# Gate logarithms summed by one fp16 product, rewritten instruction orders, and a setup whose ternary comparisons run on GpSimd

## The reference

```python
xn = layernorm(x)
Q, K, V = heads(xn @ Wq.T), heads(xn @ Wk.T), heads(xn @ Wv.T)
g = clip(sigmoid(heads(xn) @ gw.T), 1e-6)               # one gate per token and head
log_c = clip(cumsum(log(g), axis=tokens), -30, 30)       # the gate logarithms
Gc = exp(log_c) + 1e-6
R = silu(K @ sw.T)
S = cumsum(outer(K, V) * R / Gc, axis=tokens) * Gc
attn = (Q @ S) @ Wo.T
w = clip(round(w_latent / scale), -1, 1) * scale          # ternary, scale = mean |row|
h = xn @ w_fc.T + gate * (xn @ v.T @ fast_b.T @ u.T)
ffn = (relu(h) ** 2) @ w_proj.T
out = x + attn + ffn
```

## Time and profile before

| | |
|---|---|
| median of 3 runs | 655.05 us (652.91 to 655.27) |
| the profiled execution, its own time | 652.83 us |
| its span, first to last instruction | 651.0 us |
| mean granted TensorE clock | 0.998 of full |
| PE busy | 629.2 us, 97% |
| PEld (weight loads, beside PE) | 546.5 us, 84% |
| DVE busy | 507.5 us, 78% |
| ACT busy | 435.3 us, 67% |
| POOL busy | 357.1 us, 55% |
| PE's share of the chain that ended last | 92% |

### The profile page before, as it was taken

The page is one execution under the profiler, slowest core; times in us unless marked ns, Lnnn a source line. Parts: engine busy times, 40 slices in busy tenths (PEclk is TensorE's granted clock), DMA queues, the critical chain, the costliest instruction groups (busy, mean ns, idle before and its releaser), DMA issues.

```text
span 651.0 us, 21292 instructions
## 1 busy us (share of the span) xinstructions
PE 629.2 (97%) x7734; PEld 546.5 (84%) x7734; DVE 507.5 (78%) x1245; ACT 435.3 (67%) x999; POOL 357.1 (55%) x434
## 2 busy tenths in 40 slices
PE   3889999999999999999999999999999999999997
PEld 3668888888888888888888888888888888888886
DVE  5998888878787777877778877877787777878673
ACT  2688666767666776766677676667676666767662
POOL 4766465554555555456455555645555554655355
PEclk9999999999999999999999999999999999999999
DMA  9347755666746765554567856667656465677421
GB/s 309 94 124 121 111 140 135 148 142 131 111 117 129 138 132 139 135 119 112 130 139 136 143 130 97 132 136 129 143 130 135 106 125 128 141 128 127 100 45 34
DMA packets 186793, 83.05 MB, mean 128 GB/s; under 512 B 118320, under 2 KB 186160, under 8 KB 186688
## 3 DMA queue, kind: packets, MB, share of 16 engines
q1 hardware_dynamic: 184448, 79.05, 58.3%
q10 hardware_dynamic: 2240, 2.62, 1.2%
HBM read 12.43 MB, written 8.39 MB: 32 GB/s over the span
## 4 chain that ended last, share of the span: by engine, by line
PE 92%; DMA 3%; SPq 2%; DVE 1%; issue 1%; POOL 0%; POOLq 0%; DVEq 0%
PE y_bank L2251 17%; PE attn_bank L2195 9%; PE hid_b L2230 9%; PE hid_a L2230 9%; PE front_b L2132 7%; PE y_bank L2265 7%; PE front_a L2113 6%; PE front_b L2094 6%; PE score_a L2161 5%; PE attn_bank L2209 5%; PE score_b L2161 4%; PE attn_bank L2180 3%; PE hid_a L2232 2%; PE hid_b L2232 2%; DMA x_sb<-in_x 2%
## 5 line engine op out<-in xcount | busy, mean ns | idle before, releaser
L2251 PE MATMUL y_bank<-wproj_t,sq_h 128*128 128x256 f16 x512 | 118.5, 273 | 0.0
L2251 PE MATMUL y_bank<-wproj_t,sq_l 128*128 128x256 f16 x512 | 118.5, 273 | 0.0
L1727 DVE TENSOR_TENSOR sq_l<-relu_sq,sq_h 128x512 f16<-128x512 f32 x128 | 105.3, 824 | 1.0 <-ACT relu_sq L1032 0.9
L1680 DVE TENSOR_TENSOR masked<-score_a,shapes_sb 128x512 f32<-128x512 f32 x128 | 87.0, 680 | 16.0 <-PE score_a L2161 15.9
L1680 DVE TENSOR_TENSOR masked<-score_b,shapes_sb 128x512 f32<-128x512 f32 x128 | 87.2, 681 | 11.8 <-PE score_b L2161 11.7
L666 POOL TENSOR_TENSOR state_diag<-state,state_mask 128x256 f32<-128x256 f32 x56 | 53.4, 954 | 63.6 <-DVE state L1699 63.1
L1032 ACT ACTIVATE relu_sq<-relu_sq 128x512 f32<-128x512 f32 x128 | 79.6, 623 | 9.8 <-DVE sq_l L1727 9.7
L653 POOL COPY decay_halves<-decay 128x1024 uint16<-128x1024 uint16 x32 | 33.2, 1038 | 87.3 <-ACT decay L983 87.3
L697 POOL TENSOR_TENSOR y_both<-y_both,x_sb 128x512 f32<-128x512 f32 x32 | 41.2, 1287 | 70.0 <-DVE y_both L1739 70.0
L1023 ACT ACTIVATE sq_h<-relu_sq 128x512 f16<-128x512 f32 x128 | 79.2, 620 | 0.1
L933 ACT ACTIVATE vg<-front_b 128x304 f32<-128x304 f32 x64 | 27.2, 425 | 71.9 <-PE front_b L2132 71.8
(11 more groups left out here) (189 smaller groups left out, 1662.2 us busy)
## 6 DMA issues: line engine op xcount, KB each, us to landing
q_diag<-q SPq DMA_DIRECT2D x256, 64.0 KB, 2.7
k_stack<-k SPq DMA_DIRECT2D x128, 128.0 KB, 3.8
x_sb<-in_x SPq DMA_DIRECT2D x32, 256.0 KB, 3.3
out_y<-y_both SPq DMA_DIRECT2D x32, 256.0 KB, 3.4
relu_sq<-in_w_fc ACTq DMA_DIRECT2D x1, 1024.0 KB, 11.1
pj_nat<-in_w_proj ACTq DMA_DIRECT2D x1, 1024.0 KB, 13.8
y_both<-in_w_qk ACTq DMA_DIRECT2D x1, 512.0 KB, 4.6
w_stage<-in_w_qkvz_t SPq DMA_DIRECT2D x1, 512.0 KB, 6.3
```

Source lines behind the costliest of these rows:

```text
L1680: nc.vector.tensor_tensor(masked[:, c, g].rearrange("p (h n) -> p h n", h=4), score_bank[g % 2][:].rearrange("p (h n) -> p h n", h=4), cau ...
L1727: nc.vector.tensor_tensor(sq_l[:, q], sq[:, n], sq_h[:, q], ALU.subtract).then_inc(sq_l_done, 1)
L2251: last = mm(y_bank[:, c * D:(c + 1) * D], part[:, q, at:at + P], wproj_t[:, 2 * q + i], start=(q == i == c == n == 0), stop=False, skip_gr ...
```

## The change

- **Logarithms.** `log_high` (ScalarE) and `log_low` (VectorE) split the logarithms, times 1024, into two fp16 halves in one tile. `cumulate` becomes one fp16 product of the triangular matrix against both halves, 64 columns, without the sums before. `sums_taken` (VectorE, a reduction) adds the two halves from PSUM. A DMA on SP's queue (`spread_totals`) spreads the last row of the result, the chunk totals, over all partitions. `sums_before` moves to GpSimd and adds the totals up. `clip_log` becomes two VectorE instructions: add the sums before, then clip.
- **Forms on VectorE.** The two `dens` and the clip go from `tensor_scalar` to `scalar_tensor_tensor` with a second input from SBUF.
- **Ternary setup.** VectorE's `fc_ternary` and `proj_ternary` are gone. GpSimd makes both comparisons (`fc_highs`: 8 more instructions of 256 columns, `proj_highs`: 2 more of 1024). TensorE transposes and subtracts in one go: for each of the 32 blocks one fp16 product with the identity and one with its negative, into the same place.
- **Other setup.** The first unit is transposed by TensorE in place of a DMA (`first_turned`, `first_high`, `first_low`). `columns_low` goes from VectorE to GpSimd. Three of the six big memsets go from GpSimd to VectorE. The values' weights are scaled while they are split.
- **Orders.** The lists of all five engines are new. In the repeated slot the front part works one unit further ahead (`load` 6 ahead, `turn_tokens` 5, `queries_t`, `keys`, `values_gates` 4); the prologue is longer and the epilogue shorter by as much.

```diff
 def cumulate(b, u):
-    pe.wait_ge(before_step, upto(b, u, 2, 0))
-    cum = front_a[:, 0:CH * H]
-    mm(cum, causal_sb, log_den[:].rearrange("p c h -> p (c h)"), start=True, stop=False)
-    mm(cum, ones[:], before[:, u % 2].rearrange("p c h -> p (c h)"), start=False,
+    pe.wait_ge(log_l_done, upto(b, u, 1, 0))
+    mm(front_a[:, 0:2 * CH * H], causal16[:], log16[:].rearrange("p s c h -> p (s c h)"), start=True,
        stop=True).then_inc(cum_full, 1)
...
+def spread_totals(b, u):          # SP
+    sp.wait_ge(sums_taken_done, upto(b, u, 1, 0))
+    last = chunk_sums[P - 1:P, par].rearrange("p c h -> p (c h)")
+    sp.dma_start(totals[:, par].rearrange("p c h -> p (c h)"),
+                 last.unsqueeze(1).to_broadcast([1, P, CH * H])).then_inc(totals_spread[par], 16)
...
+def sums_before(b, u):            # GpSimd
+    pool.wait_ge(totals_spread[par], turned_upto(b, u))
+    nc.gpsimd.tensor_tensor(before[:, par, 1], before[:, par, 0], totals[:, par, 0],
+                            ALU.add).then_inc(before_step, 1)
...
+    nc.gpsimd.tensor_tensor(before[:, 1 - par, 0], before[:, par, 1], totals[:, par, 1],
+                            ALU.add).then_inc(before_step, 1)
...
+def fc_highs(half):               # GpSimd
+    for t in range(HT // 2 * half, HT // 2 * half + HT // 2):
+        last = nc.gpsimd.tensor_scalar(fc_above[:, t], fc_nat[:, t], fc_scale[:, 1, t:t + 1], None,
+                                       ALU.is_gt)
...
 def fc_weights(i):
-    pe.wait_ge(fc_ternary_done, half + 1)
+    pe.wait_ge(fc_below_done, half + 1)
+    pe.wait_ge(fc_above_done, half + 1)
     for j in range(4):
-        last = nc.tensor.transpose(fc_banks[i][:, j * P:j * P + P],
-                                   fc_nat[:, 4 * half + j, t * P:(t + 1) * P], ident_sb)
+        for n, part in enumerate((fc_above, fc_below)):
+            last = mm(fc_banks[i][:, j * P:j * P + P], part[:, 4 * half + j, t * P:(t + 1) * P], ident16[:, n],
+                      start=(n == 0), stop=(n == 1))
```

More of the change, by code:

```diff
@@ L549, in prologue @@
                 load(0, 3)
-                turn_tokens(0, 0)
                 load(1, 0)
+                load(1, 1)
                 turn_tokens(0, 1)
@@ new lines, in prologue @@
+                attn_low(0, 2, 1)
+                sums_before(1, 0)
+                weigh_values(1, 0, 0)
+                attn_high(0, 3, 0)
+                split_decay(1, 0)
+                weigh_values(1, 0, 1)
+                attn_high(0, 3, 1)
+                attn_low(0, 3, 0)
+                attn_low(0, 3, 1)
+                residual(0, 2)
+                diagonal_state(1, 0, 0)
+                attn_high(1, 0, 0)
+                normalise(1, 3, 0)
+                normalise(1, 3, 1)
```

1172 lines of the change are left out of this document (664 added, 508 removed).

## The result

The changed kernel takes 664.91 us (median of 4 runs, 663.05 to 667.27), the kernel before 654.17 beside it (652.91 to 655.27): ratio 1.0172, 95% interval 1.0152 to 1.0191. It is slower, and above the forecast's range. Its profiled execution has a span of 663.8 us where the one of before had 651.0, 12.8 more.

The account below looks back on a forecast made before the run. PE was taken to bound slots 3 to 29, with waits only in setup and end. Product -8.7, setup +6.2 and end +0.9 gave -1.6 us, from 655.05 to 653.4 us; 8 in 10 range 646 to 658.5.

Parts of the forecast that it names:

- The product: `cumulate` in each unit: one fp16 product of 64 columns, priced 0.08 us, saves 0.28 us a unit, -8.7 us.
- The setup: Before the first `state_update`: GpSimd's doubled comparisons make PE wait, milestone 50.13 to 55.5 us, +6.2 us with work moved.
- The end: Epilogue: `projected(7, 3, 0)` must wait for `scale_y`, +0.9 us (0 to 1.5).
- VectorE's forms: New two-input forms of `dens` and clip on VectorE: need not help by themselves; VectorE has slack, so the sum stays.
- I put the cost at nothing, up to 0.2 us a slot: Repeated slot: added small instructions, SP's extra DMA and the longer logarithm chain stay covered, costing 0 to 0.2 us.
- Rivals 2 and 3: Slots: SP's queue or the logarithms' chain delays PE; or new orders leave PE holes, slot stays 19.09, 662; together 0.15.
- the forecast's own sign of being wrong: Repeated slots in the changed profile: a slot over 18.9 us would show the forecast wrong.
- Rival 2: Every slot: SP's queue or the logarithms' chain makes PE wait; 664 us at 0.4 us a slot; 0.15 with rival 3.
- Rival 4: Setup: PE's waits leave TensorE at its lower clock for a few us, 655 to 657 us; chance 0.10.
- Sum: Whole kernel: -8.7 + 6.2 + 0.9 = -1.6 us, giving 653.4 us; bounds of the terms -6.6 to +3.2.

Follow-up runs that it names:

- e7: Changed kernel with the setup's two-sided ternary comparisons back on VectorE, the fc ones placed early, and fp32 transposes; 669.51 us (1.0227).
- e17: e16 with the proj weights made as in the kernel before (GpSimd compares once, VectorE two-sided, fp32 transposes); 659.65 us (1.0092).
- e16: e12 with two moves in the first units: tokens of (1, 0) turned earlier on SP, `xt_high(0, 2)` behind `proj_taken(1)`; 657.65 us (1.0067).
- e12: e10 with VectorE's mask of the second bank moved ahead of `squares_low` and `write_factors`; 653.53 us (1.0004).
- e10: Changed kernel with `scores(., 0, 0)` moved behind `carried` on TensorE, and its mask behind `queries_low` and `carry_state` on VectorE; 664.20 us (1.0172).
- e11: Kernel before with only `scores(., 0, 0)` moved ahead of the second chunk's `state_update`, `values` and `carried` on TensorE; 701.57 us (1.0717).
- e14: Changed kernel with products that compute nothing put in TensorE's four idle stretches of the setup; 670.01 us (1.0241).
- e4: Kernel before with the logarithm part alone, in its own orders, `spread_totals` on SP's queue behind `stack_keys`; 716.00 us (1.0958).

## Why the prediction was wrong, step by step

- **The product**: forecast -0.28 us a unit, measured -0.33, over 31 units -10.2 for -8.7. Right, mis-sized by 1.5 us in its favour: the price of 0.08 for a small product was too high. It is 0.03 here, and the proj weights' small products, priced at 0.08 too, start 0.06 us apart (eight in 0.61 us, the last one's own length included).
- **The setup**: `state_update(0, 0, 0)` forecast at 55.5, measured 55.11; comparisons from 23.1 to 38.4, measured 22.77 to 37.2; the last proj one 51.2, measured 49.55. The numbers held, but that GpSimd's comparisons alone set them is not borne out: with the second comparisons off GpSimd it was 55.81 (e7), with two proj comparisons off it 54.74 (e17, against 55.22 in e16). Which part of the new setup's order makes the 5 us stays open. Unit 0's `attn_projected` comes 7.9 us later than before in e12, but 2.9 of these are work and not waiting: from the first state update to it PE is busy without a hole for 22.4 us, where it was 19.5, and has less left to do behind.
- **The end**: forecast +0.9, a wait of 0.79 us came. From unit 27's `attn_projected` to the span's end e12 takes 60.5 us, for 61.7, though PE has 3.0 us less to do there (busy 53.99 for 56.96); two waits, this one and 0.91 us before a `projected` at 621.2, use up the rest.
- **VectorE's forms**: no run tests them alone, and no wait of PE names the `dens`. VectorE is busy for 74% of the slots; the masks it gave late were late by its order, as e12 shows.
- **"I put the cost at nothing, up to 0.2 us a slot"** is the step that failed. Against e12 the waits cost 0.39 us a slot from unit 7 to 27 (382.97 us against 375.16), 3.7 us in the first seven (219.12 - 77.47 against 215.41 - 77.51) and 1.3 behind, 12.8 us of span. I added up SP's queue (17.0 of 18.8 us: true) and gave the logarithms' chain its 16.7 us (no wait of PE names it, though `write_factors` stood in front of the mask that was late in e10), and asked of neither whether it lay on a ring, or what stood behind it on another engine. Before, `carried` stood ahead of `scores(., 0, 0)` in the slot (317.02 and 318.66 us), and the chain from it led to the next slot's `scores` at 337.69: from the end of `carried` at 317.73 it had 20.0 us, where by e11's expectation (done at 335.6) it needed some 17.9. After, `scores` stood first, and a late transfer delayed the very release that starts the next one.
- **Rivals 2 and 3** had 0.15 together, with 664 for 0.4 us a slot and 662 for a slot that stays at 19.09; that is what came (19.15 and 664.9), and the forecast's own sign of being wrong, a slot over 18.9, came too. Rival 2 named `stack_keys` late for `scores`; that SP's length decides was half true, since it matters only on the ring. Against it I set that SP's sum stays under the slot, which is a test of throughput, not of a ring.
- **Rival 4**: the clock did fall (0.64 between 24 and 36 us, 0.73 between 36 and 50), and `keys(0, 1)` took 2.77 us. In e14 that stretch was quick and PE waited for GpSimd in its place, so the comparisons hid it.
- **Sum**: e12, the same kernel with the order mended, has the span of the kernel before. Reckoned from the first state update: +5.0 for that milestone (forecast +5.4), -8.9 of PE's work behind it (forecast -8.7 + 0.8), and +3.9 of waits, 2.2 in the first seven units and 1.7 behind unit 27 (forecast +0.9, and none in the units). That its 653.5 us are the forecast's 653.4 is in part luck: against the kernels before beside each, e12 is 0.0 where I said -1.6, with 3 us of waits too few and 1 us of saving too little. The forecast was near for a kernel whose slots have no holes, and that is not the one it was made for.

## What to carry to other kernels

When an order is rewritten, look for rings: from each wait on the bounding engine follow the data back to a buffer's release, and see whether that release stands behind the waiting instruction in the same slot; if so the chain's latency, not any engine's load, bounds the slot, and it must be well under it. Two waits can hide each other (0.7 and 1.8 us alone, 11.4 together here), so an edit that takes one away and shows nothing is no proof against it: look at what PE waits for now, and take that too. And a late chain belongs at the head of no queue: in e4 one DMA waited 5.6 us there in front of others, and an order without that wait, with earlier sums, gave back 46 of 62 us.

## What was not expected of the hardware

For a small VectorE instruction its place beside GpSimd's can matter more than its work. Groups of the changed kernel (count, then us in total and mean ns):

```profile
L1824 DVE SCALAR_TENSOR_TENSOR write_full<-decay,write_den 128x32 f32<-128x32 f32 x32 | 26.2, 818 | 0.3
L1769 DVE SCALAR_TENSOR_TENSOR gate_den<-exp_neg,den_limit 128x32 f32<-128x32 f32 x32 | 7.6, 238 | 4.9 <-ACT exp_neg L1061 4.9
```

The same groups of the kernel before:

```profile
L1611 DVE TENSOR_SCALAR gate_den<-exp_neg 128x32 f32<-128x32 f32 x32 | 26.5, 828 | 5.5 <-ACT exp_neg L944 5.5
L1660 DVE SCALAR_TENSOR_TENSOR write_full<-decay,write_den 128x32 f32<-128x32 f32 x32 | 6.9, 217 | 0.0
```

`gate_den` fell from 828 to 238 ns, with form and place both new, so that no run says which did it. `write_full`, whose form did not change, rose from 217 to 818: in its new place it starts beside GpSimd's copy of the decays (both near 288.5 us, and both 1.05 us long). By the Trainium skill ("SBUF — State Buffer", Who interferes with whom) VectorE and GpSimd share one pair of ports under an exclusive lock, taken by VectorE instructions with two SBUF inputs and also by a `tensor_scalar` in a two-port mode. `write_full`, with two inputs, agrees; the old `gate_den`, a `tensor_scalar` with one, was held up as long, and whether it ran in such a mode no view shows.

The second is the fp16 product of 64 columns with full weights, 0.03 us to its successor, as little as products on quarter-width weights.
